# The first batch of a second feed-forward stage prepared inside the attention stage: a change of order on five engines

## The chip, the cores and the metric

The kernel runs on one NeuronCore of a Trainium2 chip. A core has five engines, each with its own instruction queue: TensorE (PE, matrix products into PSUM; its weight loads are shown apart as PEld), VectorE (DVE), ScalarE (ACT), GpSimd (POOL) and SyncE (SP, which here issues all DMAs). Each queue runs in order, and engines wait for each other only by semaphores. So a waiting instruction holds up all that stands behind it on its own engine. The metric is the device time of the whole program in microseconds, the median of several runs.

## What is computed

The input x has 2 batches of 1024 tokens with 128 channels, all in fp32. Three stages follow each other, and each adds to x:

```python
x = x + 0.5 * ffn(layernorm(x))        # first feed-forward stage ("FFN")
x = x + attn(layernorm(x))
x = x + 0.5 * ffn(layernorm(x))        # second FFN, the same weights

def attn(x):                           # 16 heads of 64, causal, one shared kv and a null key
    q = split_heads(x @ Wq) * scale
    kv = concat([null_kv, x @ Wkv])
    p = softmax(where(causal_mask, -max, q @ kv.T))
    return merge_heads(p @ kv) @ Wout

def ffn(x):                            # attention of 16 heads of 8 channels, mixed experts
    pooled = x.mean(tokens)            # one gate per batch, from all of its tokens
    logits = relu(pooled @ Wg1 + bg1) @ Wg2 + bg2
    w = softmax over the two largest of 4 logits, else 0
    q, k, v = x @ sum_e(w[e] * W[e]) + bias   # for q, k and v
    return (softmax(q @ k.T / sqrt(8)) @ v) @ Wo + bo
```

The gate needs the mean over all tokens of a batch. So no projection of a batch in the second FFN can start before the attention output of that whole batch is in x. The two batches do not depend on each other.

## The kernel before, in words

The order of the work is written out by hand, one program for each engine, stage by stage: `ffn(0)`, `attention()`, `ffn(1)`.

**FFN.** A batch is normed (`norm`: statistics L842 and L845, square root L660 on ScalarE, reciprocal L853, apply L855), transposed by TensorE (L1167) and copied out by ScalarE, which also sums the tokens (L665). The gate is two small products (`gate_hidden` L1178, `gate_logits` L1183), a chain of small VectorE instructions (`gating_in` L870 to L880, `gating_out` L885 to L888) and the mixing of the expert weights (L897 to L901). `project` makes q, k (L1190, bias added by L918) and v (L1195, L924). `split` writes q and k as three bf16 parts: ScalarE makes the first (L689), GpSimd the rest of it (`split_rest` L523), ScalarE the second (L693), GpSimd the third (`split_third` L529). SyncE stores the parts to `stack_dram` (`store_part`) and loads from there, for each head, a "stack" of 48 rows (`load_stack`), whose product q k is one bf16 matmul.

A unit is one head of one batch: 16 units per batch, 32 per FFN, in groups of NB = 4. For each unit there are 8 maximum tiles (`max_tile` L1218 on TensorE, `maximum` L949 on VectorE). Their result is split by GpSimd (`max_split` L546 and L548), transposed by VectorE (`max_transpose` L943), and taken by DMA through `max_dram` into two more rows of the stack. Then there are 16 score tiles (L1233), 16 exponentials (L785) and the products with v (L1249). The maximum tiles run two units ahead of the scores. In VectorE's queue `max_transpose` of unit g stands behind the first maximum of unit g + 1, and waits for GpSimd.

**Attention.** Head pairs 0 to 7 belong to batch 0, pairs 8 to 15 to batch 1. A pair has NS = 16 steps t. In step s (numbered through all pairs) TensorE makes score tile s (`a_score_tile` L1363, L1365, L1370), then the transposes of tile s - 4 (`a_transposes` L1383), and at some steps a part of the products with the values (`a_values` L1404) or half of the next pair's queries (L1345). VectorE finds the maximum of tile s (L1021), ScalarE its exponentials (L721), VectorE the reciprocal of the sum (L1040), and GpSimd scales the tile (`normalize` L638). ScalarE and VectorE copy half of the transposed tile each (L728, L1046). L719 on ScalarE runs at t = 11 and t = 15 of a pair, and makes a good mark in time. Score tiles use two places in PSUM in turn (`S_BANK`), so that tile s + 2 waits for the exponentials of tile s. All that leaves TensorE otherwise goes through three banks in rotation (`TAKES`, `T_BANKS`): a take waits until the third one before it has been read.

**The output.** Batch 0's is made inside pairs 8 and 9, a token tile of 128 tokens at each of the eight `Y_STEPS` (`token_tile_out` L1415, L1416, added to x by L1057): eight products over the pairs and one for the null key. For batch 1 it comes after the last pair (`outputs` L1423, L1424, added to x by L1064).

**Between attention and the second FFN.** After the last pair each engine runs, in this order: norm, gate, the first half of batch 1's output, projections and split of batch 0, the second half of batch 1's output, then the store and load of the first stacks, then norm, gate, projections and split of batch 1, woven with the maximum tiles of unit 0; then the maximum tiles of unit 1, and only then the first score tile. This stretch is called the gap below.

## Time and profile before

| | |
|---|---|
| median of 3 runs | 1290.66 us (1290.0 to 1292.76) |
| the profiled execution | 1291.22 us, of which its span is 1289.5 us |
| PE busy | 1173.5 us, 91% |
| DVE busy | 1063.0 us, 82% |
| ACT busy | 941.8 us, 73% |
| POOL busy | 304.1 us, 24% |
| DMA | 69.54 MB, mean 54 GB/s |

A busy share is a mean over stages that have different limits. The slices show them: in 40 equal slices of the span, PE is at nine tenths or more nearly everywhere, except in slices 14 and 15, where the first FFN ends and attention starts, and in slices 29 and 30, where attention ends and the second FFN starts. In the attention slices VectorE and ScalarE stand at seven tenths, in the FFN slices VectorE at nine. The profile's chain of waits follows back from the last instruction what each step waited for. The rows that the prediction uses stand below in numbered groups.

### The profile page before, as it was taken

The page shows a single profiled execution, that of the slowest core. Times are in us where ns is not written, and L with a number is a line of the kernel's source. Part 1 is how long each engine was busy: PE and PEld are TensorE (multiplying, and loading weights), DVE is VectorE, ACT ScalarE, POOL GpSimd, SP SyncE. Part 2 cuts the span into 40 slices and gives each one's busy share as a digit, 9 for nine tenths or more (in the row PEclk, how much of TensorE's full clock was granted, in tenths as well). Part 3 has the DMA queues.
Part 4 walks back from the last instruction along what each step waited for, and adds up shares of the span by engine and source line. Part 5 has one row for each costly group of instructions (what it writes and reads, how often), then busy time and mean ns, then how long its engine had stood idle before and what let it go on. Part 6 is the DMA issues. An engine that isn't in the chain of part 4 may idle for free. (4 is left out here: it accounts for less than half of the span.)

```text
span 1289.5 us, 32074 instructions
## 1 busy us (share of the span) xinstructions
PE 1173.5 (91%) x10916; PEld 508.9 (39%) x10916; DVE 1063.0 (82%) x1787; ACT 941.8 (73%) x2001; POOL 304.1 (24%) x534
## 2 busy tenths in 40 slices
PE   4499999999987899999999999998769999999996
PEld 3112222222225655555666556555622222222222
DVE  6889999998987777777755777776589999999896
ACT  3169999998983677777755777775239999998894
POOL 4400000021010344444423444443330000000200
PEclk9679999999996999999999999999869999999998
DMA  4811212354210001000000000000431212245312
GB/s 112 242 27 56 66 48 54 91 87 79 70 34 25 18 18 34 18 18 18 18 18 18 17 18 18 18 18 2 147 99 47 69 46 59 69 79 91 81 45 66
DMA packets 51792, 69.54 MB, mean 54 GB/s; under 512 B 21168, under 2 KB 29296, under 8 KB 51696
## 3 DMA queue, kind: packets, MB, share of 16 engines
q1 hardware_dynamic: 51696, 68.26, 21.7%
q8 instruction: 60, 0.98, 0.3%
q14 instruction: 36, 0.29, 0.1%
HBM read 37.30 MB, written 22.54 MB: 46 GB/s over the span
## 5 line engine op out<-in xcount | busy, mean ns | idle before, releaser
L949 DVE TENSOR_REDUCE neg_max<-ps 128x1 f32<-128x1024 f32 x512 | 591.3, 1215 | 28.3 <-PE ps L1218 26.3
L785 ACT ACTIVATE arena<-ps 128x512 f32<-128x512 f32 x1024 | 545.5, 597 | 88.0 <-PE ps L1233 75.8
L1233 PE MATMUL ps<-arena 50*128 50x512 bf16 x1024 | 324.9, 389 | 16.8 <-ACT arena L785 9.9
L1249 PE MATMUL ps<-arena 128*32 128x256 f32 (+1 forms) x3584 | 317.4, 426 | 8.5 <-ACT arena L785 3.1
L1218 PE MATMUL ps<-arena 48*128 48x512 bf16 x1024 | 298.2, 398 | 15.4 <-DVE neg_max L949 14.4
L1021 DVE TENSOR_REDUCE a_neg_max<-ps 128x1 f32<-128x129 f32 (+7 forms) x256 | 191.8, 749 | 115.3 <-PE ps L1370 114.3
L638 POOL TENSOR_SCALAR arena<-arena,a_rsum 128x128 f32<-128x128 f32 (+7 forms) x256 | 192.0, 750 | 320.8 <-DVE a_rsum L1040 314.4
L721 ACT ACTIVATE arena<-ps,a_neg_max 128x129 f32<-128x129 f32 (+7 forms) x256 | 189.4, 740 | 50.8 <-DVE a_neg_max L1021 38.4
L1365 PE MATMUL ps<-arena 64*128 64x128 f32 (+6 forms) x512 | 192.9, 458 | 0.0
L1363 PE MATMUL ps<-arena 64*128 64x321 f32 (+7 forms) x512 | 188.3, 451 | 4.7 <-DVE neg_s_null L1052 1.9
L1233 PEld LDWEIGHTS ps<-arena 50*128 50x128 bf16 x1024 | 74.0, 94 | 297.2 <-ACT arena L785 266.8
L728 ACT ACTIVATE arena<-ps 128x64 f32<-128x64 f32 (+7 forms) x256 | 104.2, 407 | 81.8 <-PE ps L1383 79.9
L1383 PE MATMUL ps<-ident,arena 64*128 64x64 f32 x2304 | 140.6, 228 | 9.7 <-DVE arena L1046 4.5
L1383 PEld LDWEIGHTS ps<-ident,arena 64*128 64x128 f32 x2304 | 129.3, 139 | 42.5 <-issue 26.9
L1404 PE MATMUL ps<-arena 128*64 128x512 f32 (+3 forms) x768 | 144.4, 498 | 1.3 <-DVE arena L1046 0.8
L1249 PEld LDWEIGHTS ps<-arena 128*32 128x32 f32 x3584 | 71.2, 108 | 166.6 <-issue 92.4
L546 POOL CAST max_parts<-neg_max 128x8 bf16<-128x8 f32 x64 | 12.3, 192 | 512.6 <-DVE neg_max L949 512.6
L1046 DVE COPY arena<-ps 128x64 f32<-128x64 f32 (+7 forms) x256 | 115.3, 450 | 7.6 <-PE ps L1383 5.2
L1363 PEld LDWEIGHTS ps<-arena 64*128 64x128 f32 x512 | 77.5, 190 | 81.8 <-issue 52.1
L1365 PEld LDWEIGHTS ps<-arena 64*128 64x128 f32 x512 | 78.6, 192 | 0.0
L1218 PEld LDWEIGHTS ps<-arena 48*128 48x128 bf16 x1024 | 58.0, 95 | 36.5 <-DVE neg_max L949 26.6
L1404 PEld LDWEIGHTS ps<-arena 128*64 128x64 f32 x768 | 47.0, 136 | 50.3 <-issue 38.6
(130 smaller groups left out, 827.0 us busy)
## 6 DMA issues: line engine op xcount, KB each, us to landing
arena<-stack_dram SPq DMA_DIRECT2D x128, 192.0 KB, 3.4
stack_dram<-arena SPq DMA_DIRECT2D x48, 256.0 KB, 3.6
o_dram<-arena SPq DMA_DIRECT2D x32, 256.0 KB, 2.1
arena<-arena SPq DMA_DIRECT2D x32, 256.0 KB, 3.5
arena<-o_dram SPq DMA_DIRECT2D x30, 256.0 KB, 4.3
arena<-max_dram SPq DMA_DIRECT2D x256, 1.0 KB
x<-in_L_attn_x SPq DMA_DIRECT2D x2, 512.0 KB, 5.2
max_dram<-max_T SPq DMA_DIRECT2D x64, 8.0 KB, 1.7
```

What stands on the lines that cost most here:

```text
L638: nc.gpsimd.tensor_scalar(a_probs[:, t % RING, 1:n], a_probs[:, t % RING, 1:n], a_rsum[:, t:t + 1], 1.0, ALU.mult, ALU.mult).then_inc(a_no ...
L721: nc.scalar.activation(a_probs[:, t % RING, c0:c0 + a_keys(t)], a_region(t), ACT.Exp, bias=a_neg_max[:, t:t + 1], accum_out=a_sum[:, t:t + ...
L785: nc.scalar.activation(probs[:, t, :], ps[:, EXP_BANK[t], :], ACT.Exp, scale=F_SCALE).then_inc(probs_ready, 1)
L949: nc.vector.tensor_reduce(neg_max[:, g, t:t + 1], ps[:, bank:bank + 2, :].rearrange("p a b -> p (a b)"), AX, ALU.max, negate=True).then_in ...
L1021: ins = nc.vector.tensor_reduce(a_neg_max[:, t:t + 1], a_region(t), AX, ALU.max, negate=True)
L1218: ins = nc.tensor.matmul(ps[:, bank + h, :], stack[rows, g, 0, t * P:(t + 1) * P], stack[rows, g, 1, h * HALF:(h + 1) * HALF], start=True, ...
L1233: ins = nc.tensor.matmul(ps[:, bank, :], stack[rows, g, 1, kt * P:(kt + 1) * P], stack[rows, g, 0, h * HALF:(h + 1) * HALF], start=True, s ...
L1249: ins = nc.tensor.matmul(ps[row:row + 32, PV_BANK, cols], v_unit[:, g, t // 2, :], probs[:, t, cols], start=j == 0 and c0 == 0 and g % 2 == 0,
L1363: nc.tensor.matmul(ps[:, mid, HALF - split + head:HALF], q_s[0:AD, par, hh, cols], k_f[0:AD, b, k0 + head:k0 + split], start=True, stop=True)
L1365: nc.tensor.matmul(ps[:, mid + 1, 0:n - split], q_s[AD:P, par, hh, cols], k_f[AD:P, b, k0 + split:k0 + n], start=True, stop=False)
L1383: ins = nc.tensor.transpose(ps[:, TAKE_BANK["T", NS * pg + t, half], j * ROWS:(j + 1) * ROWS], a_probs[rows, t % RING, 1 + j * P:1 + (j + ...
L1404: ins = nc.tensor.matmul(ps[hh * AD:(hh + 1) * AD, PV_BANK, q0:HALF], av[:, pg // PAIRS, kt, :], probs_T[qh][:, hh, kt, q0:HALF], start=kt ...
```

## The change

The work is the same but for the null key's row. Its place in the program differs.

- **Batch 0 of the second FFN goes into pairs 10 to 14** (`early_batch` on VectorE and ScalarE, `early_take` on TensorE, `early_rest` and `early_third` on GpSimd, `store_early` on SyncE). Statistics and norm are in pair 10, transposes ("N") and gate ("G") in pair 11, the q projections ("J") and v ("W") in pair 12, the k projections in pair 13. The two halves of q are split in pair 12, those of k in pairs 13 and 14. The ten new takes join the rotation of three banks. Each is read by VectorE or ScalarE in the step behind it.
- **The stacks of units 0 and 1 are loaded in pair 15**, after a smaller memset on GpSimd. Seven of unit 0's maximum tiles stand in the steps behind the last score tile (`MAX_STEPS`), then its last one and the first of unit 1.
- **Batch 1's output is summed over seven pairs early**, in eight token tiles: four at steps 4, 8, 10 and 12 of pair 15, four in the steps behind its last score tile. The eighth pair's share follows at the end (`last_outputs`), two products of four tiles each.
- **The null key's row** is made on all 128 partitions (`null_values` with a weight of 128 columns where it had 16), and GpSimd adds it to x in pair 1 (`add_null`). The ninth product of each token tile goes.
- In `ffn(1)` only batch 1 is left to prepare, woven with the maximum tiles of unit 1.

In TensorE's queue before, at the end of attention (L1383 transposes, L1404 products with the values, L1167 norm transposes, L1178 and L1183 gate, L1423 output):

```order
L1383 MATMUL ps<-ident,arena 128x64 x42
L1404 MATMUL ps<-arena 64x512 x10
L1404 MATMUL ps<-arena 64x384 x2
L1404 MATMUL ps<-arena 64x256 x2
L1404 MATMUL ps<-arena 64x128 x2
L1167 MATMUL ps<-ident,xn 128x128 x8
L1178 MATMUL ps<-tok_sum,wg 128x1 x2
L1183 MATMUL ps<-wg,hid 128x4
L1423 MATMUL ps<-wout,arena 128x128 x8
```

And in the changed kernel (L1549 transposes, L1582 seven-pair output, L1374 maximum tiles, L1570 products with the values):

```order
L1549 MATMUL ps<-ident,arena 128x64 x12
L1582 MATMUL ps<-wout,arena 128x128 x7
L1374 MATMUL ps<-arena 128x512 x2
L1549 MATMUL ps<-ident,arena 128x64 x14
L1582 MATMUL ps<-wout,arena 128x128 x7
L1374 MATMUL ps<-arena 128x512 x2
L1549 MATMUL ps<-ident,arena 128x64 x16
L1582 MATMUL ps<-wout,arena 128x128 x7
L1374 MATMUL ps<-arena 128x512 x2
L1582 MATMUL ps<-wout,arena 128x128 x7
L1570 MATMUL ps<-arena 64x512 x4
L1374 MATMUL ps<-arena 128x512 x2
```

The norm and gate of batch 0 have left this place. Output tiles and maximum tiles stand between the last transposes and the products with the values.

In VectorE's queue before, in the gap (L1064 adds the output to x, L918 and L924 take the projections, L842 to L855 norm, L949 maxima, L870 the gate):

```order
L1064 TENSOR_TENSOR x<-ps,x 128x512
L918 TENSOR_SCALAR arena<-ps,b_mix 128x512 x4
L924 TENSOR_TENSOR arena<-ps,w_mix 128x16x8 x8
L1064 TENSOR_TENSOR x<-ps,x 128x512
L842 BN_STATS stats<-x 128x6 x8
L845 BN_AGGR mean_var<-stats 128x2 x8
L853 RECIPROCAL rstd<-rstd 128x8
L855 TENSOR_SCALAR xn<-x,mean_var,rstd 128x128 x8
L949 TENSOR_REDUCE neg_max<-ps 128x1 x3
L870 TENSOR_TENSOR lg<-ps,bg 128x4
```

And in the changed kernel, from the end of attention on (L1173 and L1180 add to x, L1064 maxima, L1058 transpose, L941 to L954 norm, L970 the gate):

```order
L1173 TENSOR_TENSOR x<-ps,x 128x128 x2
L1064 TENSOR_REDUCE neg_max<-ps 128x1 x6
L1180 TENSOR_TENSOR x<-ps,x 128x512 x2
L941 BN_STATS stats<-x 128x6 x8
L944 BN_AGGR mean_var<-stats 128x2 x8
L1064 TENSOR_REDUCE neg_max<-ps 128x1
L1058 STREAM_TRANSPOSE max_T<-max_parts 128x32
L1064 TENSOR_REDUCE neg_max<-ps 128x1
L952 RECIPROCAL rstd<-rstd 128x8
L954 TENSOR_SCALAR xn<-x,mean_var,rstd 128x128 x8
L1064 TENSOR_REDUCE neg_max<-ps 128x1 x2
L970 TENSOR_TENSOR lg<-ps,bg 128x4
```

The maxima of unit 0 now stand ahead of the norm of batch 1, and those of unit 1 in it.

In ScalarE's queue of the changed kernel, in pair 10 (L808 exponentials, L815 copies, L732 square root):

```order
L808 ACTIVATE arena,a_sum<-ps,a_neg_max 128x641
L815 ACTIVATE arena<-ps 128x2x64
L808 ACTIVATE arena,a_sum<-ps,a_neg_max 128x769
L732 ACT_TABLE_LOAD
L732 ACTIVATE rstd<-mean_var,eps_col 128x8
L815 ACTIVATE arena<-ps 128x3x64
L808 ACT_TABLE_LOAD
L808 ACTIVATE arena,a_sum<-ps,a_neg_max 128x897
```

The square root brings two table loads between the exponentials of steps 9 and 10.

```diff
         Y_STEPS = [NS * PAIRS + k for k in (8, 10, 12, 14)] + [NS * PAIRS + NS + k for k in (2, 8, 10, 12)]
+        Y_STEPS += [NS * (N_PAIRS - 1) + k for k in (4, 8, 10, 12, 17, 18, 19, 20)]
+        MAX_STEPS = [NS * N_PAIRS + k for k in (1, 2, 3, 5, 9, 11, 13)]
+        EARLY_STEPS = {}
+        for kind, pair, steps in (("N", PAIRS + 3, (0, 2)), ("G", PAIRS + 3, (4, 6)), ("J", PAIRS + 4, (2, 6)),
+                                  ("W", PAIRS + 4, (10, 14)), ("J", PAIRS + 5, (8, 12))):
+            for k, t in enumerate(steps):
+                EARLY_STEPS[NS * pair + t] = (kind, k if kind != "J" else k + 2 * (pair - PAIRS - 4), 0)
...
+            def store_early(k):
+
+                sp.wait_ge(part3_ready, 4 * B + 2 * k + 2)
+                for p, pair in enumerate(PRODUCTS):
+                    sp.dma_start(stack_dram.ap()[0:FH, p, :, k, :], parts_q[:, pair[k], :]).then_inc(parts_stored, 16)
...
+            def early_rest(c):
+
+                s = slice(c % 2 * HALF, (c % 2 + 1) * HALF)
+                pool.wait_ge(part1_ready, 4 * B + c + 1)
+                nc.gpsimd.tensor_tensor(early[:, c % 2, :], early[:, c % 2, :], parts_q[:, 0, s], ALU.subtract).then_inc(rest_ready, 1)
+
...
+            def add_null(b, g):
+
+                pool.wait_ge(xn_ready, 2 * (B + b) + 2)
+                if b == 0 and g == 0:
+                    pool.wait_ge(null_ready, 1)
+                xs = x[:, b * NT + 4 * g:b * NT + 4 * g + 4, :]
+                nc.gpsimd.tensor_tensor(xs, xs, null_out[:, :].unsqueeze(1).broadcast_to([P, 4, C]), ALU.add).then_inc(null_added, 1)
...
                         normalize(i, t)
+                for pg in range(PAIRS + 4, N_PAIRS):
+                    for t in range(NS):
+                        for c in range(4):
+                            if NS * pg + t == EARLY_REST[c]:
+                                early_rest(c)
+                            if NS * pg + t == EARLY_SECOND[c]:
+                                early_third(c)
+                        if (pg, t) == (N_PAIRS - 1, 4):
+                            pool.wait_ge(a_scores, NS * (N_PAIRS - 1))
+                            nc.gpsimd.memset(stack[:, 0:2, 1, :], 1.0).then_inc(stacks_clear, 1)
+                        normalize(pg, t)
...
+            def early_first(c):
+
+                s = slice(c % 2 * HALF, (c % 2 + 1) * HALF)
+                act.wait_ge(qkf_ready, 4 * B + c + 1)
+                if c % 2 == 0:
+                    act.wait_ge(parts_stored, 16 * len(PRODUCTS) * (2 * B + c // 2))
+                nc.scalar.activation(parts_q[:, 0, s], early[:, c % 2, :], ACT.Copy).then_inc(part1_ready, 1)
...
+                def early_batch(s):
+                    if s == NS * (PAIRS + 2) + 9:
+                        norm_std(2 * B, 0)
+                    if s - 1 in EARLY_STEPS:
+                        kind, k, _ = EARLY_STEPS[s - 1]
+                        if kind == "N":
+                            norm_T_half(2 * B, 0, k, TAKE_BANK["N", k, 0])
+                        elif (kind, k) == ("G", 0):
+                            hidden(B, TAKE_BANK["G", 0, 0])
+                    if s - 2 in EARLY_STEPS and EARLY_STEPS[s - 2] == ("G", 1, 0):
+                        gate_exp(B)
+                    for c in range(4):
+                        if s == EARLY_REST[c]:
+                            early_first(c)
+                        if s == EARLY_SECOND[c]:
+                            early_second(c)
 
...
+            def project_early(c):
+
+                dve.wait_ge(qk_done, 4 * B + c + 1)
+                if c >= 2:
+                    dve.wait_ge(part3_ready, 4 * B + c - 1)
+                nc.vector.tensor_scalar(early[:, c % 2, :], ps[:, TAKE_BANK["J", c, 0], :], b_mix[:, 0, c // 2:c // 2 + 1], None,
+                                        ALU.add).then_inc(qkf_ready, 1)
...
+                def early_batch(s):
+                    t = s - NS * (PAIRS + 2)
+                    if 0 <= t < NT:
+                        if t == 0:
+                            dve.wait_ge(x_ready, 2 * B + 2)
+                        ins = nc.vector.bn_stats(stats[:, t, :], x[:, t, :])
+                        if t == NT - 1:
+                            link(ins)
+                            for k in range(NT):
+                                ins = nc.vector.bn_aggr(mean_var[:, k, :], stats[:, k, :])
+                            ins.then_inc(mv_ready, 1)
+                    if t == 11:
+                        dve.wait_ge(std_ready, 2 * B + 1)
+                        dve.wait_ge(xT_done, 4 * B)
+                        link(nc.vector.reciprocal(rstd[:, 0:NT], rstd[:, 0:NT]))
+                    if 12 <= t < NS:
+                        for k in range(2 * t - 24, 2 * t - 22):
+                            ins = nc.vector.tensor_scalar(xn[:, k, :], x[:, k, :], mean_var[:, k, 0:1], rstd[:, k:k + 1],
+                                                          ALU.subtract, ALU.mult)
+                        if t % 2:
+                            ins.then_inc(xn_ready, 1)
+                    if s - 1 in EARLY_STEPS:
+                        kind, k, _ = EARLY_STEPS[s - 1]
...
+                            gating_in(B, 0, TAKE_BANK["G", 1, 0])
+                        elif kind == "J":
+                            project_early(k)
+                        elif kind == "W":
+                            project_v(B, 0, k, TAKE_BANK["W", k, 0])
+                    if s - 3 in EARLY_STEPS and EARLY_STEPS[s - 3] == ("G", 1, 0):
+                        gate_weights(B, 0)
+                    if s - 4 in EARLY_STEPS and EARLY_STEPS[s - 4] == ("G", 1, 0):
+                        mix_expert(0, 0)
+                    for e in range(1, E):
+                        if s - 4 - e in EARLY_STEPS and EARLY_STEPS[s - 4 - e] == ("G", 1, 0):
+                            mix_expert(0, e)
+
                 for s in range(LAST_STEP + 1):
                     pg, t = divmod(s, NS)
...
-                norm(2 * B, 0)
-                gating(B, 0)
-                add_out(B - 1, 0, 0)
-                project(B, 0)
-                add_out(B - 1, 1, 1)
+                    early_batch(s)
+                    if s in MAX_STEPS:
+                        maximum(0, UNITS // NB, MAX_STEPS.index(s), EARLY_MAX_BANK)
+
+                maximum(0, UNITS // NB, NT - 1, EARLY_MAX_BANK)
...
+                    max_transpose(0, i0)
+                    maximum(1, i0, 2)
+                    norm_apply(2 * B + 1, 1)
+                    maximum(1, i0, 3)
+                    maximum(1, i0, 4)
                     gating_in(B + 1, 1)
-                    maximum(0, i0, 3)
+                    maximum(1, i0, 5)
                     gating_out(B + 1, 1)
-                    maximum(0, i0, 4)
...
+                        pe.wait_ge(gexp_in if n else hid_ready, B + 1)
+                    elif kind == "J":
+                        pe.wait_ge(qkf_ready, 4 * B + n + 1)
+                    elif kind == "W":
+                        pe.wait_ge(v_ready, 2 * B + n + 1)
                     else:
                         pe.wait_ge(evac_dve if k else evac_act, n + 1)
 
...
+                n = PAIRS if k < NT else PAIRS - 1
+                pe.wait_ge(pv_bank_free, (2 * PAIRS if k < NT else 2 * (N_PAIRS - 1)) - 1 + k % NT // 4)
                 wait_taken(("Y", k, 0))
-                bank, tok = TAKE_BANK["Y", k, 0], slice(k * P, (k + 1) * P)
-                for p in range(PAIRS):
-                    nc.tensor.matmul(ps[:, bank, 0:C], o_T[:, p, tok], wout[:, p, :], start=p == 0, stop=False)
-                nc.tensor.matmul(ps[:, bank, 0:C], ones[:, :], null_out[:, :], start=False, stop=True).then_inc(ay_done, 1)
-
...
+            def early_take(kind, k):
+
+                wait_taken((kind, k, 0))
+                bank = TAKE_BANK[kind, k, 0]
+                if kind == "N":
+                    norm_T_half(2 * B, k, bank)
+                elif kind == "G" and k == 0:
+                    gate_hidden(2 * B, B, 0, bank)
+                elif kind == "G":
+                    gate_logits(B, 0, bank)
+                elif kind == "J":
+                    pe.wait_ge(mix_ready, B + 1)
+                    project_qk(B, 0, k, bank)
+                else:
+                    project_v(B, 0, k, bank)
+
...
+            def last_outputs(g):
 
                 for t in range(4):
                     tok = slice((4 * g + t) * P, (4 * g + t + 1) * P)
-                    for p in range(PAIRS):
-                        nc.tensor.matmul(ps[:, bank, t * C:(t + 1) * C], o_T[:, p, tok], wout[:, p, :], start=p == 0, stop=False)
-                    ins = nc.tensor.matmul(ps[:, bank, t * C:(t + 1) * C], ones[:, :], null_out[:, :], start=False, stop=True)
+                    ins = nc.tensor.matmul(ps[:, OUT_BANK[g], t * C:(t + 1) * C], o_T[:, PAIRS - 1, tok], wout[:, PAIRS - 1, :],
+                                           start=True, stop=True)
                 ins.then_inc(ay_done, 1)
...
                     if query_half(s):
                         queries(query_half(s)[0], query_half(s)[0] // PAIRS, query_half(s)[1])
+                    if s in EARLY_STEPS:
+                        early_take(*EARLY_STEPS[s][0:2])
                     if s in Y_STEPS:
                         token_tile_out(Y_STEPS.index(s))
+                    if s in MAX_STEPS:
+                        k = MAX_STEPS.index(s)
+                        if k < 2:
```

## Rows read from the trace of the kernel before

**Rows 1.** windows (us; busy PE, PEld, DVE, ACT, POOL; PEclk): one pair, the gap

```profile
574.89:602.88 27.99, 27.51 (x294) 16.45 (x292) 20.82 (x55) 20.94 (x54) 12.00 (x16) 1.00 0.08 20
894.47:961.50 67.03, 48.52 (x261) 31.10 (x261) 45.27 (x111) 19.58 (x36) 19.57 (x23) 0.78 0.35 106
952.00:960.00 8.00, 4.35 (x16) 1.00 (x17) 8.00 (x9) 0.08 (x1) 4.02 (x4) 0.50 0.41 122
```

**Rows 2.** timeline of ScalarE, one mark (L719) in pair 7 and in pair 10

```profile
631.03 0.29 ACT L719 ACTIVATE sum_null<-neg_s_null,a_neg_max 128x1 f32<-128x1 f32 x1 [0.28 <-DVE a_neg_max L1025]
...
735.77 0.29 ACT L719 ACTIVATE sum_null<-neg_s_null,a_neg_max 128x1 f32<-128x1 f32 x1 [0.28 <-DVE a_neg_max L1025]
```

**Rows 3.** timeline of TensorE in the gap, one token tile's output

```profile
900.09 2.05 PE L1423 MATMUL ps<-wout,arena 128*128 128x128 f32 x16
902.08 0.48 PE L1424 MATMUL ps<-null_out,ones 16*128 16x128 f32 x2
902.49 2.05 PE L1423 MATMUL ps<-wout,arena 128*128 128x128 f32 x16
```

**Rows 4.** timeline of TensorE: next pair's queries in pair 9 and in pair 6

```profile
685.67 1.12 PE L1345 MATMUL ps<-xnT,wq 128*128 128x512 f32 x2 [1.06 <-DVE x L1057]
...
588.23 1.12 PE L1345 MATMUL ps<-xnT,wq 128*128 128x512 f32 x2
```

**Rows 5.** timeline of VectorE and ScalarE at step 3 of pair 6

```profile
588.34 0.69 DVE L1046 COPY arena<-ps 128x512 f32<-128x512 f32 x1
...
588.80 0.68 ACT L721 ACTIVATE arena<-ps,a_neg_max 128x513 f32<-128x513 f32 x1
```

**Rows 6.** timeline of TensorE in the gap, the first-batch work

```profile
894.40 1.09 PE L1167 MATMUL ps<-ident,xn 128*128 128x128 f32 x8
896.41 0.61 PE L1178 MATMUL ps<-tok_sum,wg 128*128 128x1 f32 x4 [0.92 <-ACT xnT L665]
...
907.28 3.70 PE L1190 MATMUL ps<-xnT,w_mix 128*128 128x512 f32 x8
910.82 1.95 PE L1195 MATMUL ps<-w_mix,xnT 128*128 128x128 f32 x16
```

**Rows 7.** timeline of TensorE, end of attention, and one maximum tile at full clock

```profile
888.66 5.81 PE L1404 MATMUL ps<-arena 128*64 128x512 f32 x32 [0.79 <-DVE arena L1046]
...
947.96 0.39 PE L1218 MATMUL ps<-arena 48*128 48x512 bf16 x2
```

**Rows 8.** timeline of VectorE in the gap, the second batch's norm to the first transpose

```profile
922.91 1.65 DVE L842 BATCH_NORM_STATS2 stats<-x 128x6 f32<-128x128 f32 x8
...
925.84 2.14 DVE L855 TENSOR_SCALAR xn<-x,mean_var,rstd 128x128 f32<-128x128 f32 x8
...
933.14 0.15 DVE L870 TENSOR_TENSOR lg<-ps,bg 128x4 f32<-128x4 f32 x1
...
939.23 0.75 DVE L901 SCALAR_TENSOR_TENSOR w_mix<-w_experts,gate,w_mix 128x512 f32<-128x512 f32 x1
...
942.21 0.75 DVE L918 TENSOR_SCALAR arena<-ps,b_mix 128x512 f32<-128x512 f32 x1 [1.09 <-issue]
...
952.49 9.10 DVE L949 TENSOR_REDUCE neg_max<-ps 128x1 f32<-128x1024 f32 x8
...
961.50 0.20 DVE L943 STREAM_TRANSPOSE max_T<-max_parts 128x32 bf16<-128x32 bf16 x1
```

**Rows 9.** timeline of GpSimd in the gap

```profile
910.07 4.52 POOL L523 TENSOR_TENSOR arena<-arena 128x512 f32<-128x512 f32 x4 [18.79 <-ACT arena L689]
...
960.80 0.19 POOL L546 CAST max_parts<-neg_max 128x8 bf16<-128x8 f32 x1 [4.78 <-DVE neg_max L949]
```

**Rows 10.** timeline of ScalarE in pair 0, around a square root

```profile
412.70 1.28 ACT L660 ACT_TABLE_LOAD   x1
...
414.31 1.28 ACT L721 ACT_TABLE_LOAD   x1
```

**Rows 11.** timeline of VectorE at the start, the same norm beside GpSimd memsets

```profile
8.29 2.88 DVE L855 TENSOR_SCALAR xn<-x,mean_var,rstd 128x128 f32<-128x128 f32 x8
```

273 lines of the change are left out of this document (158 added, 115 removed).

## The prediction, made before the changed kernel ran

> **What bounds the kernel now.** I read the slices first, for where TensorE (PE) falls below nine tenths, then windows of those stretches, then the timeline engine by engine, and the order of the changed queues last. The windows are to show that attention and the gap have different limits [rows 1]. In a stretch of 27.99 us, from step 11 of one pair to step 11 of the next, PE is busy for 27.51 us at the full clock of 2.4 GHz, VectorE (DVE) for 20.82 and ScalarE (ACT) for 20.94. So attention is bound by PE: what PE gets there in addition costs its own length, and each wait put before PE costs its length too, since only 0.48 us a pair is free. The gap runs from the last product with the values, at 894.47, to the transpose at 961.50 that stands behind the first maximum of unit 2. From there VectorE sets the pace with eight maxima a unit. The gap takes 67.03 us, in which no engine is busy all the time, at a mean clock of 0.78: it is a chain of handovers.
>
> The price of PE work in attention can be read where it was tried. Pairs 8 and 9 hold the eight token tiles of batch 0. Between the same mark in pair 7 and in pair 10 lie 104.74 us [rows 2], three pair lengths are 83.97, so the eight tiles cost 20.77 us, 2.60 each. PE needs 1.99 us for a tile's sixteen rows of products and 0.41 for the null key's, 2.40 in all [rows 3], 19.2 for eight. Of the 1.57 us beyond that, 1.06 is one wait: the queries at step 3 of pair 9 wait for VectorE's add of the token tile that was taken at step 2 [rows 4]. The rest is 0.06 a tile.
>
> **What the early work costs in pairs 8 to 15, up to the last score tile.**
>
> 1. Null key's product gone from batch 0's tiles: 8 x 0.41 = -3.3 us [rows 3]. GpSimd's four adds instead stand in pair 1, beside work that leaves GpSimd 16 us of 28 free [rows 1]; I cost them at nothing. Uncovered they would be four of about 1.13 us, by the price of one subtraction [rows 9].
> 2. Four seven-pair tiles in pair 15: 7/8 x 1.99 = 1.74, and 0.06, 1.8 each: +7.2. No queries stand in pair 15 to wait for them.
> 3. Norm transposes 1.09, gate 0.61 and about 0.4 for the logits, q and k 3.70, v 1.95 [rows 6]: +7.7.
> 4. The four waits that the rotation of three banks brings. A take at step 2 or 6 of a pair holds the bank that the queries at step 3 or 7 want. Its reader stands at the very end of the next step on its engine, behind the maximum or the exponentials of that step. In pairs 11 and 12 this happens four times: second transposes, logits, first and second q projection. Pair 9 gives the measure: 1.06 us with a reader of 0.28 us. With a q projection's reader of 0.75 us [rows 8] it is 1.06 + 0.47 = 1.5, twice. The gate chain is nine small instructions, the first of them 0.15 us [rows 8]; with the waits between them I estimate 1.5, so 1.06 + 1.2 = 2.3. The transposes' reader is ScalarE: at step 3 the exponentials end at 589.48, a copy of 0.6 follows, and the queries, which start at 588.23 in an undisturbed pair [rows 4, 5], wait until about 590.2: 2.0. Together +7.3. Bounds: 0, if the engines have drawn ahead by then, and 9. I take 7.3, since the nearest row shows such a wait in full.
> 5. The square root in pair 10 puts two table loads of 1.28 us [rows 10] and the root of 0.3 between two exponentials. ScalarE has about 1.0 us of slack at that place and a score tile waits two steps later; I take 1.1, between 0 and 2.9.
> 6. VectorE's own additions in pairs 10 to 13: 1.65 + 0.64 statistics, 2.14 apply, 1.5 + 0.8 gate, 3.6 mixing, four q and k readers 3.0, v 1.7, some 15 us over four pairs in which it has 7.2 us each free. The apply and the mixing stand at the long steps 10 to 15, where it is nearly full. I take 1.5, between 0 and 5.
> 7. GpSimd: eight halves of about 1.13 us and a memset; one delays a scaling that the transposes need, 0.4. The null key's product at the start of attention gets weights of 128 columns where it had 16, at the low clock on the path: 0.4 (0 to 1). Together +0.8.
>
> Sum up to the last score tile: -3.3 + 7.2 + 7.7 + 7.3 + 1.1 + 1.5 + 0.8 = +22.3 us.
>
> **The end of attention and the gap.** Behind the last score tile PE had little to do but wait: each transposes-to-copy handover leaves it 0.7 to 0.8 us idle (0.79 in the row), several times, and then come the values' products, 5.81 us [rows 7]. Now PE also has four tiles, 4 x 1.74 = 7.0, and seven maximum tiles, 7 x 0.39 = 2.7. Two of the output tiles wait for the bank of the tile before, and that add stands on VectorE behind a maximum (1.14 us, 9.10 / 8 [rows 8]), a copy and itself: 1.7 us each, 3.4. Of the old idle time 2.5 is filled. The last product with the values ends 7.0 + 2.7 + 3.4 - 2.5 = 10.6 us later.
>
> From there the chain to the same transpose, each piece from the rows of before: three maxima and two adds to x with their handovers 5.6; statistics, apply, two maxima and a transpose 7.4; transposes, copies and gate products until the logits are read 4.2 (927.98 to 933.14 is 5.2, of which I give 1.0 to the third maximum that VectorE had to finish first); gate chain, one maximum, mixing 6.8 (933.14 to 939.98); until the first q is read 2.2; the other three projections 4.6 (each 3.70 / 4 = 0.93 at the full clock, twice that at the low one: two low, one full); copy of 0.6, hand over and first subtraction of 1.1 for the last 2.0; four second subtractions 4.5, like the four first; split and transpose 0.9 (960.80 to 961.70) [rows 8, 9]. That is 38.2 us in place of 67.03. Before, that transpose never waited for GpSimd; now it is the last thing on the chain, since GpSimd does batch 1's third parts ahead of unit 1's split. VectorE stands for some 2.5 us there. That is in the sum.
>
> One thing comes back: before, PE ran at 1.2 GHz from 952 to 960 and into unit 0 [rows 1], and the first interval between such transposes was longer than later ones by about 1 us. Now PE is busier just before; I take 0.6 of it. The gap saves 67.0 - 38.2 - 10.6 + 0.6 = 18.8 us.
>
> **The sum.** +22.3 - 18.8 = +3.5 us on the profiled execution's 1291.22, which lies 0.56 above the median: 1294.2 as a median. What happens before pair 8 and after the gap is the same work in the same order.
>
> A rule of the Trainium skill speaks to item 5. The rows show that the second load begins 1.61 us after the first began, with the root between them [rows 10]: a load and the root fill that, and nothing else. "ScalarE: Activation LUTs", section "What ACT_TABLE_LOAD costs", gives 1283 ns for a load and a drain of about 1380 ns with each switch. By that the two switches would take 5.6 us with the root, and the sum would be up to 2.7 us higher, 1296.9. The rows have no room for the drain here, so the sum stays with them.
>
> **Rivals.**
>
> A. The interleaved work fits in (faster). Attention takes only PE's own work, and the waits of items 4 to 6 vanish because each engine, given PE's extra time, has drawn ahead. For it: seven of the eight tiles in pairs 8 and 9 brought almost no wait. Against it: the one that stood a step before queries brought 1.06 us. Items 4 to 6 fall from 9.9 to 1.5: 1294.2 - 8.4 = 1285.8 us. It decides as soon as the four waits are under 0.9 us each.
>
> B. The clock (no change). The part after attention now is shorter and denser, so PE could hold 2.4 GHz in it. The q and k projections would take 1.9 less, the transposes and gate products 1.0, the first unit 0.6: 1294.2 - 3.5 = 1290.7. For it: the old gap's mean of 0.78 was not all low, and the work in it is now denser. Against it: maximum tiles that wait for VectorE kept it at 0.50 in 952 to 960, while it was busy for 4.35 of 8 us [rows 1], and the same pattern stands before the new gate.
>
> C. VectorE and GpSimd in each other's way (slower still). The norm's apply of 2.14 us took 2.88 at the start of the program, where GpSimd's memsets ran beside it [rows 11]: 0.74 more for eight instructions. In pair 10 they stand two by two in four long steps beside GpSimd's longest scalings, and in pair 11 the mixing does. If each of the four couples waits like that, 3.0, and half as much again in pair 11, 1.5: 1294.2 + 4.5 = 1298.7 us. It decides where VectorE's slack at those steps is used up. Against it: in pair 0 the same apply took its 2.14 beside lighter scalings.
> The Trainium skill has the rule to it, "SBUF — State Buffer", section "Who interferes with whom": a VectorE instruction in a two-port mode, or with two SBUF inputs against a GpSimd read, and a GpSimd instruction hold a shared pair of ports for a whole instruction, and the other is fully blocked. The 2.88 us agrees.
>
> **How the numbers follow.** My case has 0.42, its own range 1290.5 to 1297.5 (item 4 at 4 to 9, items 5 and 6 at 1 to 5). A has 0.24, B 0.16, C 0.18. This kernel's runs tell a change from none at about 0.2%, 2.6 us: no change is 1288.1 to 1293.2. My case lies above that with 0.28 of its 0.42, the rest within; A is faster but for 0.02; B is within but for 0.01 on either side; C is slower. That gives faster 0.23, same 0.30, slower 0.47. The range of 1285.5 to 1299 takes in A's value and C's and leaves their far halves out.
>
> **What would show it.** In the changed trace: the mark that was L719, from pair 7 to pair 10 at 101.4 us (104.74 - 3.3); pairs 10 to 12 longer than 27.99, pair 11 by 2.1 of work and over 4 of waits, with queries that name ScalarE's or VectorE's early readers as releaser; the last product with the values 33 us later than 894.5 (22.3 + 10.6); 38 us from there to the transpose behind unit 2's first maximum, and VectorE idle before it for GpSimd. Queries that start without a wait in pairs 11 and 12 would prove item 4 wrong and A right. A gap of under 34 us at full clock would prove B. Applies of over 0.3 us each in pair 10 would speak for C.

## The result, and the profile after

The changed kernel takes 1293.4 us in the median of 12 runs, the kernel before 1290.11 in the median of 12 on the same chip. The ratio of their runs is 1.0031, with a 95% interval of 1.0015 to 1.0046: slower by about 0.3%. One run of the twelve, 1432.86 us at a mean clock of 0.738, is left out of that ratio; without it the median is 1293.24. The profiled execution took 1291.37 us (span 1289.6), the lowest of the twelve.

Windows of the trace after, cut at the marks of the pairs (step 11 of pairs 10, 11, 12, 13, 14, 15), at the end of the last product with the values and at the transpose behind unit 2's first maximum. They answer to [rows 1], where a pair takes 27.99 us and the gap 67.03.

```profile
727.92:765.63 37.71, 31.61 (x310) 18.84 (x312) 25.92 (x77) 22.70 (x61) 11.97 (x16) 0.95 0.06 15
765.63:800.53 34.90, 30.45 (x304) 17.52 (x300) 24.99 (x63) 22.55 (x57) 15.39 (x19) 1.00 0.07 17
800.53:831.52 30.99, 30.22 (x306) 17.54 (x302) 23.25 (x64) 21.48 (x55) 13.14 (x17) 1.00 0.23 69
831.52:861.55 30.03, 28.95 (x296) 16.83 (x294) 22.51 (x56) 22.70 (x59) 16.51 (x20) 1.00 0.19 52
861.55:893.42 31.87, 30.91 (x332) 20.55 (x330) 20.05 (x55) 20.30 (x52) 13.75 (x17) 1.00 0.17 45
893.42:924.99 31.57, 28.07 (x272) 18.08 (x268) 17.78 (x34) 10.79 (x22) 9.87 (x15) 1.00 0.11 26
924.99:962.52 37.53, 21.85 (x96) 11.02 (x95) 28.88 (x74) 13.63 (x25) 9.82 (x12) 0.69 0.01 1
```

The gap is 29.5 us shorter. Attention has paid for it: the first of these stretches holds 31.61 us of TensorE in 37.71, so over 6 us of waiting stand in a stretch that had 0.48 free, and its clock of 0.95 says that part of the rest ran at 1.2 GHz.

The marks in pairs 7 and 10, as in [rows 2]:

```profile
624.95 0.30 ACT L806 ACTIVATE sum_null<-neg_s_null,a_neg_max 128x1 f32<-128x1 f32 x1 [0.28 <-DVE a_neg_max L1140]
727.92 0.29 ACT L806 ACTIVATE sum_null<-neg_s_null,a_neg_max 128x1 f32<-128x1 f32 x1
```

They are 102.97 us apart, in place of 104.74. TensorE's waits in pairs 11 and 12, as in [rows 4]:

```profile
740.86 0.65 PE L1549 MATMUL ps<-ident,arena 64*128 64x64 f32 x14 [1.17 <-ACT xnT L737]
745.20 1.12 PE L1511 MATMUL ps<-xnT,wq 128*128 128x512 f32 x2 [1.88 <-ACT xnT L737]
754.74 1.84 PE L1511 MATMUL ps<-xnT,wq 128*128 128x512 f32 x2 [2.36 <-DVE g_s L980]
782.10 1.12 PE L1511 MATMUL ps<-xnT,wq 128*128 128x512 f32 x2 [1.52 <-DVE arena L1032]
790.81 1.13 PE L1511 MATMUL ps<-xnT,wq 128*128 128x512 f32 x2 [1.50 <-DVE arena L1032]
```

The four rows of L1511 are the queries. What releases them is ScalarE's copy of the normed input (L737), the last step of the gate's first half on VectorE (L980) and the readers of the first two q projections (L1032). In the tail two output tiles wait for VectorE's add:

```profile
909.63 1.80 PE L1582 MATMUL ps<-wout,arena 128*128 128x128 f32 x14 [1.71 <-DVE x L1173]
913.96 1.80 PE L1582 MATMUL ps<-wout,arena 128*128 128x128 f32 x14 [1.72 <-DVE x L1173]
```

At the end of the gap VectorE stands for GpSimd, which does four third parts of 1.12 us first; [rows 8, 9] had no such wait:

```profile
957.13 4.49 POOL L561 TENSOR_TENSOR arena<-arena 128x512 bf16<-128x512 f32 x4
961.91 0.19 POOL L578 CAST max_parts<-neg_max 128x8 bf16<-128x8 f32 x1 [0.29 <-POOL arena L561]
```

```profile
962.52 0.21 DVE L1058 STREAM_TRANSPOSE max_T<-max_parts 128x32 bf16<-128x32 bf16 x1 [3.38 <-POOL max_parts L580]
```

### The profile page after: what moved, and what is told of

The parts are those of the page before. It is cut to its first block and busy times, and to the rows that moved or that the text cites. A ratio compares the mean times of both kernels' runs of the same rounds, so it can differ in the third digit from the quotient of the medians.

```text
span 1289.6 us, 31942 instructions
## 1 busy us (share of the span) xinstructions
PE 1165.2 (90%) x10884; PEld 502.7 (39%) x10884; DVE 1066.6 (83%) x1795; ACT 942.0 (73%) x2001; POOL 308.4 (24%) x536
## 5 line engine op out<-in xcount | busy, mean ns | idle before, releaser
L1064 DVE TENSOR_REDUCE neg_max<-ps 128x1 f32<-128x1024 f32 x512 | 592.1, 1219 | 33.4 <-PE ps L1374 31.6
L1374 PE MATMUL ps<-arena 48*128 48x512 bf16 x1024 | 294.7, 392 | 17.0 <-DVE neg_max L1064 16.0
L808 ACT ACTIVATE arena<-ps,a_neg_max 128x129 f32<-128x129 f32 (+7 forms) x256 | 189.8, 741 | 52.9 <-DVE a_neg_max L1136 42.7
L815 ACT ACTIVATE arena<-ps 128x64 f32<-128x64 f32 (+7 forms) x256 | 104.4, 408 | 92.0 <-PE ps L1549 90.4
L1549 PE MATMUL ps<-ident,arena 64*128 64x64 f32 x2304 | 139.8, 228 | 9.8 <-DVE arena L1161 3.4
L1549 PEld LDWEIGHTS ps<-ident,arena 64*128 64x128 f32 x2304 | 128.5, 139 | 44.7 <-issue 28.2
L1570 PE MATMUL ps<-arena 128*64 128x512 f32 (+3 forms) x768 | 145.0, 498 | 0.5 <-DVE arena L1146 0.4
L1374 PEld LDWEIGHTS ps<-arena 48*128 48x128 bf16 x1024 | 57.9, 94 | 35.9 <-DVE neg_max L1064 25.4
L1570 PEld LDWEIGHTS ps<-arena 128*64 128x64 f32 x768 | 46.7, 136 | 48.6 <-issue 37.7
```

What stands on the lines that cost most here:

```text
L808: nc.scalar.activation(a_probs[:, t % RING, c0:c0 + a_keys(t)], a_region(t), ACT.Exp, bias=a_neg_max[:, t:t + 1], accum_out=a_sum[:, t:t + ...
L1064: nc.vector.tensor_reduce(neg_max[:, g, t:t + 1], ps[:, bank:bank + 2, :].rearrange("p a b -> p (a b)"), AX, ALU.max, negate=True).then_in ...
L1374: ins = nc.tensor.matmul(ps[:, bank + h, :], stack[rows, g, 0, t * P:(t + 1) * P], stack[rows, g, 1, h * HALF:(h + 1) * HALF], start=True, ...
L1549: ins = nc.tensor.transpose(ps[:, TAKE_BANK["T", NS * pg + t, half], j * ROWS:(j + 1) * ROWS], a_probs[rows, t % RING, 1 + j * P:1 + (j + ...
L1570: ins = nc.tensor.matmul(ps[hh * AD:(hh + 1) * AD, PV_BANK, q0:HALF], av[:, pg // PAIRS, kt, :], probs_T[qh][:, hh, kt, q0:HALF], start=kt ...
```

## The experiments

This table is worked out from the traces: the mark in pair 7, then the lengths from there to the mark in pair 10, to the mark in pair 15, to the end of the last product with the values (the tail), to the transpose behind unit 2's first maximum (the gap), and to the last such transpose. "Ratio" is to the kernel before, measured beside it. The medians come from several sets of runs, in which the kernel before itself stood at 1288.3 to 1290.1, so differences of medians between rows are good to about 2 us; where they and the ratios disagree, both are given.

```
kernel                    p7      7-10    10-15   tail   gap    after   median   ratio (95%)
before                  631.03  104.74  139.26  19.44  67.03  292.54  1290.11  1
changed                 624.95  102.97  165.50  31.57  37.53  292.12  1293.4   1.0031 (1.0015-1.0046)
e1 takes apart          624.84  102.94  162.12  31.56  37.42  291.79  1289.61  0.9992 (0.9973-1.0011)
e2 split first          626.41  102.93  165.36  31.56  34.17  291.73  1288.76  0.9981 (0.9965-0.9997)
e3 maxima later         624.60  102.94  165.48  31.44  37.64  292.84  1291.51  1.0025 (1.0005-1.0045)
e4 null only            627.24  101.44  139.25  19.44  64.08  293.41  1281.68  0.9930 (0.9904-0.9955)
e5 null's prep. only    627.04  104.74  139.23  21.13  68.49  291.57  1289.37  0.9999 (0.9984-1.0014)
e6 null + outputs       624.32  101.44  144.00  27.99  66.23  291.22  1294.81  1.0047 (1.0032-1.0063)
e7 null + early FFN     629.03  102.93  165.92  21.42  49.41  291.75  1292.16  1.0005 (0.9988-1.0023)
e8 e1 + e2              624.25  102.93  162.17  31.56  34.04  290.99  1283.38  0.9952 (0.9934-0.9970)
e9 readers first        626.11  101.81  155.65  30.44  36.90  291.11  1279.56  0.9940 (0.9919-0.9961)
e10 e8 + mixing spread  626.14  102.95  158.98  31.56  33.89  290.69  1281.18  0.9953 (0.9934-0.9972)
e11 all moves           624.73  101.79  157.17  30.42  34.17  290.73  1276.9   0.9916 (0.9896-0.9937)
e12 readers + split     625.22  101.80  155.63  30.43  33.34  292.49  1276.11  0.9908 (0.9894-0.9922)
```

**e1_takes_apart: is it the step of the take?**

```
-"N" (0, 2)  "G" (4, 6)   "J" pair 12 (2, 6)    EARLY_REST 5, 9
+"N" (0, 4)  "G" (8, 10)  "J" pair 12 (4, 8)    EARLY_REST 7, 11
```

> The changed kernel with the early transposes, gate products and the first two q projections taken at steps 0 and 4, 8 and 10, 4 and 8, where no queries stand at the next step; everything else as it was. Theory (the rotation of three banks makes the queries wait for a reader at the end of the step): the four waits of 1.88, 2.36, 1.52 and 1.50 us before the queries of pairs 11 and 12 go, and pairs 11 and 12 are 6 to 7 us shorter together; a wait of a few tenths may come in their place before transposes two steps on. Some 1287 us, 0.995 of the changed kernel. Rival (the four waits only show where VectorE and ScalarE are behind anyway, so the same time comes up as other waits in the same pairs): pairs 11 and 12 stay within 2 us of what they are, 1292 to 1294 us.

The four waits are gone and pair 10 to 11 takes 31.35 us in place of 37.71, but pair 11 to 12 takes 37.40 in place of 34.90: with the gate four steps later, the mixing falls into steps 14 to 17. The two together are 3.9 us shorter, for a forecast of 6 to 7; net 3.4 us from pair 10 to 15 in the trace, 3.8 in the medians. The theory holds for the waits; the price of the new place was not in it. Part of that price is the clock:

```profile
770.00:775.00 5.00, 3.19 (x60) 2.63 (x58) 4.93 (x13) 2.66 (x9) 2.51 (x3) 1.00 0.02 3
775.00:780.00 5.00, 4.77 (x12) 1.88 (x12) 2.78 (x9) 2.89 (x9) 1.68 (x3) 0.52 0.00 0
```

VectorE, with the mixing in it, is busy for 4.93 of 5 us; TensorE gets only 3.19, in waits of 0.30, 0.90 and 0.84 us, and its granted clock is 0.52 in the next 5 us and 0.80 in the 5 after. So in this trace the fall of the clock has moved from pair 11 to the start of pair 12, and has not gone.

**e2_split_first: the gap's last link**

```
                 split_rest(ph * B + 1)
+                if ph == 1:
+                    max_split(1, ph * UNITS + 1)
                 split_third(ph * B + 1)
```

> The changed kernel with GpSimd's split of unit 1's maxima placed ahead of batch 1's four third parts instead of behind them. Theory (the last link of the chain in the gap is GpSimd, VectorE stands 3.4 us for it): the transpose behind unit 2's first maximum comes 3.3 us earlier and the time falls by 3 to 5 us, to about 1289, the more so as TensorE no longer stands still around it. Rival (the next thing is late anyway, the third parts or the stacks stored from them): the transpose is earlier, but the ones after it, by the sixth, are where they were; 1292 to 1294 us.

The gap falls by 3.36 us, the wait of 3.38, and what follows it does not grow. The theory holds; the medians' 4.6 is a little more than the link, and what makes the rest is not shown.

**e3_maxima_later: the tail**

```
-MAX_STEPS = [... for k in (1, 2, 3, 5, 9, 11, 13)]
+MAX_STEPS = [... for k in (4, 5, 6, 8, 9, 11, 13)]
```

> The changed kernel with the first four interleaved maximum tiles of unit 0 behind the last score tile moved from steps 1, 2, 3, 5 to 4, 5, 6, 8, so that VectorE's adds for the output tiles at steps 2 and 3 have no maximum ahead of them. Theory (the two output tiles at 909.63 and 913.96 us wait 1.71 and 1.72 us because a maximum of 1.2 us stands before the add that frees their bank): both waits fall under 0.6 us and the last product with the values comes 2 to 3 us earlier; about 1291 us. Rival (TensorE waits in that stretch for the exponentials and scalings of the last tiles in any order, and the maxima come late at the end): no gain or up to 1 us slower, 1293 to 1295 us.

TensorE's waits in the tail of this kernel:

```profile
908.37 1.80 PE L1582 MATMUL ps<-wout,arena 128*128 128x128 f32 x14 [1.03 <-DVE x L1173]
911.91 3.36 PE L1582 MATMUL ps<-wout,arena 128*128 128x128 f32 x28 [1.10 <-DVE x L1173]
919.11 0.39 PE L1374 MATMUL ps<-arena 48*128 48x512 bf16 x2 [1.11 <-DVE neg_max L1064]
```

The two waits are 0.7 shorter each, and a maximum tile between the values' products now waits 1.11. The tail is 0.1 us shorter: for it the rival holds. The median of 1291.51 is the theory's, but the ratio of 1.0025 (1.0005 to 1.0045) is not to be told from the changed kernel's 1.0031, and from pair 7 on its trace is 0.6 us longer. VectorE's add still stands behind the next copy, and that, I think, is what the 1.0 left is.

**e4_null_only: the null row by itself**

The kernel before with the hunks of null_wide, null_out, add_null and the missing ninth product, and no others.

> The kernel before with the null row's part of the change alone: the row of all pairs comes out on 128 rows, GpSimd adds it to x in pair 1, and the output tiles lose their ninth product. Theory: the eight tiles in pairs 8 and 9 lose 8 x 0.41 = 3.3 us, the eight in the gap up to as much where they are on the path; nothing before pair 8 changes by more than 0.5 us. 1290.1 - 4.5 = 1285.6 us. Rival (the changed kernel's trace showed only 2.9 us less between the marks in pairs 7 and 9, and its first pair came 5.8 us earlier than before in work that the change hardly touches: if that is an effect of the null row's new preparation, it shows here too): the mark in pair 1 comes near 457 instead of 462.8 us, and the time is under 1282 us.

TensorE in its gap, eight pairs' products for four tiles, where before they took 9.56 us (897.72 to 907.28) with the null key's:

```profile
890.62 7.39 PE L1435 MATMUL ps<-wout,arena 128*128 128x128 f32 x64
```

The marks 7 and 10 are 101.44 us apart, 3.30 less, as the eight products of 0.41 (3.28) have it. The gap gives another 2.95. This part of the change alone makes the kernel 7.8 us faster than the kernel before, measured beside it, so the rest of the change costs 11.7 (13.0 by the ratios). My theory had 4.5 and missed 3.3 of it. The rival's time (under 1282) came, but its cause is refuted by the next experiment; from pair 7 on the traces account for 5.4, and where the rest of the 7.8 lies is open. The mark in pair 1 stood at 458.98, near neither value named.

**e5_prep_only: was the early mark the change's doing?**

```
-nc.gpsimd.memset(ones[:, :], 1.0)
+nc.gpsimd.memset(ones[:, :], 0.0)      (with the null row's preparation and adds, and the ninth product kept)
```

> The kernel before with the null row's preparation and GpSimd's four adds of it in pair 1, while the output tiles keep their ninth product, now of zeros, so that only what stands ahead of pair 8 differs from before. The kernel with the whole of the null row's part ran in 1281.7 us, 7.8 under before, and its trace accounts for 3.3 in pairs 8 and 9 and 3.0 in the gap. Theory (the products account for it, and the start of before's one trace was late by the clock's doing): within 0.2% of before, 1288 to 1291 us, and the mark in pair 1 comes anywhere from 456 to 463 us. Rival (the preparation itself makes the first FFN or the start of attention shorter): 1285 to 1287 us.

0.9999, with an interval of 0.0015 either way: no effect above 2 us. So the 6.08 us by which pair 7's mark came earlier in the changed kernel's trace are not the change's; in the work that is the same in both, before's one trace ran longer at 1.2 GHz: its mean granted clock was 0.66 from 30 to 90 us and 0.76 from 380 to 430, where the changed kernel's was 0.72 and 0.80. The marks of these traces scatter by 6.8 us. This execution had a low stretch of its own: its last product with the values took 7.50 us, where [rows 7] has 5.81.

**e6_null_and_outputs: the early output tiles alone**

Step e4 and the second line of Y_STEPS, token_tile_out with n pairs, and one pair's product in the gap.

> The kernel before with the null row's part and the early output tiles of seven pairs, but with all of the FFN's first-batch work in the gap as before, and without maximum tiles in the tail. Against the null row's part alone (1281.7 us): four tiles in pair 15 cost 7.2 us, four in the tail 7.0 and two waits of about 1.1 less 2.5 of filled idle time; the gap's outputs shrink from two of 7.3 us to two of about 1. Theory (TensorE is on the path at both places, so its work costs the same here and there, and the waits come on top): 7.2 + 6.7 - 12.5, about 1.4 us more, 1283 us. Rival (the moved products pay off, since the tail's idle time and the clock hide them): 1279 us or less. Other rival (they carry most of what the whole change loses against the null row alone): over 1287 us.

```profile
907.34 5.82 PE L1203 MATMUL ps<-xnT,w_mix 128*128 128x512 f32 x8 [4.64 <-DVE w_mix L912]
914.77 1.06 PE L1438 MATMUL ps<-wout,arena 128*128 128x128 f32 x8
921.60 2.05 PE L1180 MATMUL ps<-ident,xn 128*128 128x128 f32 x8 [5.77 <-DVE xn L866]
931.92 1.04 PE L1231 MATMUL ps<-arena 48*128 48x512 bf16 x4 [8.28 <-DMA arena<-stack_dram]
```

My theory failed by 12 us; the second rival (over 1287) came out. Attention and the tail cost 13.3 us more than in e4, about as forecast (4.75 and 8.55; I had 13.9), but the gap did not shrink by 12.5: it grew by 2.15. Where the output products stood, TensorE now waits 4.64 us for the mixing and 8.28 us for unit 0's stack, and between them the q and k products, 3.70 us in [rows 6], take 5.82 at a granted clock of 0.50 to 0.84. In the gap the outputs had filled the time in which batch 0's gate, its splits and the way of its stacks through memory ran. They cost almost nothing there.

**e7_null_and_early_ffn: the early FFN work alone**

```
-Y_STEPS += [NS * (N_PAIRS - 1) + k for k in (4, 8, 10, 12, 17, 18, 19, 20)]
```

and all eight pairs' products in the gap.

> The changed kernel without the early output tiles of batch 1: pair 15 and the tail hold none, and the two output groups stand in the gap with all eight pairs; the FFN's early work and the interleaved maximum tiles stay. Theory (the early FFN work with its bank waits carries most of the 11.7 us that the changed kernel loses against the null row's part alone): attention keeps 20 us of extra time up to pair 15, the gap gets 15 us shorter than with the null row alone; 1281.7 + 6 to 10, so 1288 to 1292 us. Rival (the loss is that of the output tiles and their waits): 1282 to 1285 us.

The median is 10.5 us above e4, just over the 6 to 10 of the theory, and in the trace attention is 26.7 us longer than in e4, not 20. The traced execution is the highest of its 11 (1297.06; they spread from 1287.11). In it, behind the first long wait of pair 11, TensorE ran for some 20 us at a low clock. The spread goes with the clock: the six executions above 1292 us have a mean granted clock of 0.955 to 0.959, the five below 1290 of 0.960 to 0.965. Where the others lost it, one trace can't tell.

```profile
745.00:750.00 5.00, 3.12 (x42) 2.16 (x41) 1.99 (x4) 2.95 (x8) 0.51 (x2) 1.00 0.00 0
750.00:755.00 5.00, 4.98 (x27) 3.21 (x28) 2.04 (x8) 2.37 (x8) 1.65 (x3) 0.54 0.01 2
755.00:760.00 5.00, 4.19 (x34) 2.18 (x30) 1.94 (x6) 1.70 (x5) 0.48 (x1) 0.77 0.02 3
760.00:765.00 5.00, 3.45 (x11) 1.45 (x12) 2.14 (x11) 1.05 (x3) 0.25 (x1) 0.57 0.00 0
```

The gap is 49.41 us, 14.7 less than in e4. So with the null row in, either half of the rest costs 13.1 and 10.5 us, and both together only 11.7. The gaps show where they meet: against e4's 64.08 us the output tiles alone leave it 2.15 longer, the early FFN work alone 14.67 shorter, and both 26.55 shorter. I read it as two chains side by side, of which each alone leaves the other standing.

**e8_apart_and_split**

The edits of e1 and e2.

> The changed kernel with both: the early takes at steps without queries behind them, and GpSimd's split of unit 1 ahead of the third parts. Alone they ran in 1289.6 and 1288.8 us against 1293.4. Theory (two waits at different places, their gains add): 1293.4 - 3.8 - 4.6 = 1285.0 us. Rival (the second is partly the clock, or the runs' scatter): 1287 to 1289 us.

The gains add: 1283.38, and by the ratios 0.9952 where the two alone make 0.9942. Its stretch from pair 11 to 12 takes 37.5 us, and as in e1 TensorE's granted clock is 0.50 in it from 775 to 780. VectorE in it, and GpSimd:

```profile
768.19 0.21 DVE L1003 SCALAR_TENSOR_TENSOR b_mix<-b_experts,gate,b_mix 128x2 f32<-128x2 f32 x1
769.77 0.72 DVE L1003 SCALAR_TENSOR_TENSOR b_mix<-b_experts,gate,b_mix 128x2 f32<-128x2 f32 x1
```

```profile
769.46 1.01 POOL L675 TENSOR_SCALAR arena<-arena,a_rsum 128x896 f32<-128x896 f32 x1 [2.00 <-DVE a_rsum L1157]
```

A mixing instruction of 0.21 us took 0.72 where it began inside a scaling of GpSimd's, and ended at 770.49, as the scaling did at 770.47. It is no single case: the next one, of 0.62 us at 772.24, ends at 772.86 with the scaling of 771.74 to 772.86, and in e1's trace two more (0.71 at 770.36, 0.62 at 772.83) end within 0.02 us of a scaling's end.

**e9_readers_first: the reader's place**

```
                         query_1(...)
+                    if s - 1 in Y_STEPS:
+                        add_token_tile(Y_STEPS.index(s - 1))
+                    early_readers(s)
                     if 0 <= s - 2 < NS * N_PAIRS:
                         a_recip(*divmod(s - 2, NS))
                     ... a_maximum, a_evac ...
-                    if s - 1 in Y_STEPS:
-                        add_token_tile(Y_STEPS.index(s - 1))
-                    early_batch(s)
+                    early_norm(s)
```

and on ScalarE the copies of the early transposes and the gate's first step likewise right behind query_0.

> The changed kernel with the takes at their steps, but with the readers of the early takes and the adds of the output tiles placed where the queries' readers stand, at the head of the next step on VectorE and ScalarE, instead of behind that step's maximum, exponentials and copies. Theory (the waits last as long as what stands ahead of the reader on its engine): the four waits of 1.88, 2.36, 1.52 and 1.50 us and the two of 1.71 and 1.72 in the tail fall to 0.5 or less, and batch 0's of 1.06 goes; of those 11 us some 2 to 3 come back, since the maxima and exponentials now start later by the length of the readers. 1293.4 - 8 = 1285.4 us. Rival (delaying the maxima costs as much as the banks did): 1291 to 1294 us.

TensorE's waits at the queries of pairs 11 and 12 and at the tail's output tiles, all that are left:

```profile
750.39 1.13 PE L1517 MATMUL ps<-xnT,wq 128*128 128x512 f32 x2 [0.94 <-DVE g_s L980]
...
899.24 1.80 PE L1588 MATMUL ps<-wout,arena 128*128 128x128 f32 x14 [1.18 <-DVE x L1173]
902.97 1.80 PE L1588 MATMUL ps<-wout,arena 128*128 128x128 f32 x14 [1.12 <-DVE x L1173]
```

1279.56 us, 13.8 below the changed kernel (11.7 by the ratios) and more than the 8 expected; against the kernel before, 0.9940. Three of the four waits are gone, batch 0's of 1.06 too, and the 2 to 3 us that I expected back do not show; but the tail's two fell only to 1.18 and 1.12, not to 0.5, since a maximum still stands ahead of the add there. Between the marks of pairs 10 and 15 the trace is 9.85 us shorter, the tail 1.13, batch 0's tiles 1.16. The 9.85 is more than the waits of 7.26, of which 0.94 is still there, and two more rows show why. First the changed kernel, then this one, the same 10 us of pair 11 (pair 10's mark is at 727.92 in both):

```profile
750.00:755.00 5.00, 2.64 (x31) 2.04 (x30) 3.23 (x14) 2.17 (x6) 0.48 (x1) 1.00 0.01 3
755.00:760.00 5.00, 5.00 (x24) 2.29 (x25) 2.71 (x6) 1.87 (x6) 1.27 (x2) 0.66 0.31 68
```

```profile
750.00:755.00 5.00, 4.61 (x28) 2.17 (x28) 4.60 (x15) 3.15 (x9) 1.77 (x3) 1.00 0.31 70
755.00:760.00 5.00, 5.00 (x45) 2.67 (x45) 4.10 (x12) 2.42 (x8) 1.71 (x2) 1.00 0.10 34
```

With the waits TensorE was busy for 2.64 of 5 us, and in the next 5 its granted clock was 0.66: 24 matmuls. Without them it stayed at 2.4 GHz: 45, in part of other sizes. The waits had a second price behind them. An estimate from these rows: 5 us at 0.66 hold 1.7 less work than at full clock; with the 7.5 of waits that went (1.17 at 740.86 is one of them) that is 9.2 of the 9.85.

**e10_mixing_spread**

```
+MIX_STEPS = [NS * (PAIRS + 4) + t for t in (0, 1, 2, 4)]     "J" pair 12 (8, 12)
```

> The kernel with the takes apart and GpSimd's split first (1283.4 us), with the mixing of the weights moved from steps 14 to 17 behind pair 11's start, at pair 12's steps 0, 1, 2 and 4, and the first two q projections from steps 4 and 8 to 8 and 12. In that kernel's trace the stretch from pair 11 to pair 12 takes 37.5 us in place of 28, of which 2.8 is the moved work; VectorE is busy without a break in it from 758.3 to 775.8 us. Theory (VectorE is the bound in that stretch, with the mixing in the longest steps): the stretch and its neighbours together fall by 3 to 4 us, 1279.8 us. Rival (it is GpSimd that holds VectorE up there, or the bank waits return at other steps): under 1 us of gain, 1282.5 to 1284 us.

From pair 10 to 15 the trace is 3.2 us shorter than e8's, but the ratios are 0.9953 and 0.9952. The timed runs show no gain, so the theory is not borne out. The low clock of e8's trace (0.50 from 775 to 780, 0.84 from 780 to 785) is not in this one; by these figures it is worth some 3.3 us, an estimate, which is enough for the 3.2. Whether e8's other executions had it is not known.

**e11_all_moves**

The edits of e1, e2, e9 and e10.

> The changed kernel with all four moves: readers first, takes apart, mixing spread, GpSimd's split first. Theory: on top of the kernel with the last three it saves the two waits in the tail (3.4 us) and batch 0's (1.06), of which about 1 comes back; some 3 us below that kernel, 1277 us. Rival (the reader's place and the takes' places do the same thing twice, and TensorE's clock or idle time in the tail takes the rest): no better than that kernel by more than 1 us.

1276.9 us: 4 us below e10, and the tail is 1.1 us shorter and batch 0's tiles 1.2, as the theory has it.

**e12_readers_and_split**

The edits of e2 and e9.

> The changed kernel with two moves, readers first and GpSimd's split first, the takes and the mixing at their old steps. Alone, readers first ran in 1279.6 us and the split in 1288.8, against 1293.4. Theory (the split's link at the end of the gap is independent of what attention does, and with the readers first the takes' steps no longer matter): 1279.6 - 4.6 = 1275.0 us, below the kernel with all four moves (1276.9). Rival (the takes' places still matter beside it): 1277 to 1279 us.

1276.11 us, a ratio of 0.9908 (0.9894 to 0.9922): 1.1 above what the sum of gains gives, 0.9 below the rival's lowest, and not to be told from e11. In the trace the stretch from pair 10 to 15 is 155.63 us, in e11 157.17: once the readers stand first, moving the takes and the mixing too brings nothing. Its gap is 33.34 us. It beats the changed kernel by over 1% and the kernel before by 0.9%; against the null row alone (0.9904 to 0.9955) it is ahead by 5.6 us in the medians and by 0.0022, 2.8 us, in the ratios, and the two intervals overlap. Some 1.2 us of that is batch 0's tiles with their adds first, which the null row alone could have too. So the whole loss of 11.7 us comes back with the readers' places and one order on GpSimd; that the early work is then worth more than the null row alone is not shown.

## Why the prediction was right, step by step

The forecast was 1294.2 us, slower; measured, 1293.4. The four waits of item 4 were there, at their places and in their sizes, and with the readers first (e9), which takes most of them away, the change is faster than before. Moving the takes (e1) takes all four away too, but brings the time only to that of the kernel before. But the sum met the median partly by luck.

- Item 1, the null key's product: -3.3 forecast, -3.30 measured (e4).
- Items 2 and 3, tiles and moved work: in e6 three of the four tiles before pair 15's mark cost 4.75, 1.6 each, where I had 1.8. The 7.7 of moved work I have no run for by itself; e9's 16.4 us from pair 10 to 15 above before's leaves 11.6 beside the tiles for it and items 4 to 7.
- Item 4: four waits of 1.88, 2.36, 1.52 and 1.50 are 7.26, forecast 7.3 (2.0, 2.3, 1.5, 1.5). The size of the term was still too small. Removing most of their cause gave 9.85: TensorE's transposes waited another 1.17 at 740.86, and the clock fell behind the waits (0.66), which I had weighed for the gap alone, never for a wait inside attention.
- Item 5: between the marks of pairs 7 and 10, the changed kernel is 1.53 us behind e4, for a forecast of 1.1; VectorE's statistics are in that too. The mark that the prediction named as a sign, 101.4 us, had left this term of its own sum out; it came at 102.97. The rows are those of [rows 10]:

```profile
723.53 1.28 ACT L732 ACT_TABLE_LOAD   x1
724.82 0.30 ACT L732 ACTIVATE rstd<-mean_var,eps_col 128x8 f32<-128x8 f32 x1
725.03 0.31 ACT L815 ACTIVATE arena<-ps 128x192 f32<-128x192 f32 x1
725.36 1.28 ACT L808 ACT_TABLE_LOAD   x1
```

The second load begins 1.83 us after the first, with the root and a copy between them, and there is no room for more; the instruction ahead of the first load ends at 723.52. The drain of about 1380 ns that the Trainium skill gives in "ScalarE: Activation LUTs", section "What ACT_TABLE_LOAD costs", does not show in these rows either.

- Items 6 and 7: forecast 1.9 together, not separated by a run. Whether the 0.4 for the null row's weights of 128 columns is there can't be told from e5's time, which is known to 2 us. Its trace shows no sign of it: 15 of these products took 1.94 us, where 16 took 3.10 in the kernel before, at a lower clock.
- Up to the last product with the values, from pair 7: forecast +32.5 on before's trace (32.9 with the 0.4 that lies ahead of it), measured +36.6 (-1.8, +26.2, +12.1). The tail was forecast at 12.4 with pair 15's last tile in it and is 12.1; its two waits, 1.7 each, are 1.71 and 1.72.
- The gap chain: 38.2 forecast, 37.53 measured, with 3.38 of waiting for GpSimd where I had 2.5. Named as the last link, and e2 shows it: 34.17 without it. The pieces fit too, as the gate chain with its maximum and the mixing: 6.8 forecast, 6.9 measured (941.09 to 947.96).
- The clock's give-back of 0.6: the first interval behind the gap was 11.63 us and not shorter than before's 10.53, so the reason given is wrong; up to the last transpose the stretch is 0.42 shorter all the same.

In the two traces the part from pair 7 to the last transpose is 6.7 us longer, where I had 3.1; in the medians the change costs 3.3. The two traces as a whole differ by 0.15 us only, since before's came to pair 7 6.08 us later, much of it at the low clock. That is the luck: from pair 7 on the sum was 3.6 us short, and the medians do not show it. Which execution is typical ahead of pair 7 a trace of one each can't tell, and it stays open.

Rival A (it fits in) came out where the readers stand first, and not before: there all but one of item 4's waits are gone and the time is even under its 1285.8. Rival B is refuted: the gap's mean clock is 0.69 in the rows above, lower than before's 0.78. Rival C was not put to the test in pair 10: the four couples of applies (at 729.85, 731.95, 734.13 and 736.63) stood beside no scaling but for 0.09 us of one, and took 0.60 us each, 0.59 the last. Nor does pair 0 speak against C, as I wrote: its apply of 2.14 us ran from 414.56 in a pause of GpSimd's from 412.96 to 417.82. Pair 11's mixing in the changed kernel took its old time. The effect is real where instructions meet, as in e8's 0.72 for 0.21: it agrees with the Trainium skill, "SBUF — State Buffer", section "Who interferes with whom", by which the one waits for the other's whole instruction.

What the prediction missed is none of its terms but a comparison it never made: the parts of the change against each other. The null row alone is worth 7.8 us, and item 1 had 3.3 of it, since I counted the gap's outputs only as gone with the rest.

## What to carry to other kernels

When work is put between others through rotating buffers, place its reader on each engine first in the next step, where the readers of the buffers' other users stand, before choosing the steps; the reader's place was worth 13.8 us here, the step 3.8, with a fall of the clock in its new place. Price a wait on TensorE in a dense stretch with the clock that it may lose behind it, and expect runs to scatter. Before moving work out of a gap, ask what it covers there: here the output tiles alone left the gap 2.2 us longer, the early FFN work alone 14.7 shorter, and both together 26.6 shorter.

## What the runs showed of the hardware

TensorE's clock fell behind short waits inside dense work too, where I had expected it only in gaps. In the four traces with the waits of pair 11 the granted clock fell from 1.00 to 0.66 (the changed kernel and e2), 0.69 (e3) and 0.54 (e7) for 5 us, in e7 with more at 0.57 to 0.77 behind it. In e1 and e8 waits of 0.30, 0.90 and 0.84 us within 4 us stood ahead of a fall to 0.52 and 0.50. In e9 to e12 it stayed at 1.00 from pair 10 to 15. VectorE instructions of 0.21 us took 0.62 to 0.72 when they began inside a GpSimd scaling, and ended with it, in four cases in two traces.
